# Running a router's gelu, logits, softmax and top-2 picks inside attention, in nine groups of tiles

## The reference

```python
x = layernorm(x + attention(x))       # 4 heads of 64, rotary embedding, causal softmax, output projection
# router, on the tokens xf of the normed x
ri = concat([xf, stats(xf)], -1)      # mean, std, min, max, l2 norm, share of near-zeros: 262 columns
h = gelu(ri @ r1_w.T + r1_b, approximate=False)     # 128 hidden columns
probs = softmax(h @ r2_w.T, -1)                     # 32 experts
topp, topi = top_k(probs, 2)
wnorm = topp / topp.sum(-1)                         # the two gates of a token
score = where(routed, probs, -inf)
idx = argsort(-score, axis=0)[:320].T               # each expert takes its 320 best tokens
out = sum over experts of w * down(silu(gate) * up) of the gathered tokens, plus a grouped adapter
x = layernorm(x + out)
```

## Time and profile before

| what | us |
|---|---|
| three runs, median (lowest to highest) | 2360.45 (2357.5 to 2361.66) |
| the profiled execution, its own time | 2361.54 |
| its span, first to last instruction | 2359.6 |
| PE busy over the span | 1971.2 |
| DVE busy | 1491.6 |
| ACT busy | 1331.8 |
| POOL busy | 823.7 |
| granted PE clock, mean over the span | 0.922 |

### The profile page before, as it was taken

The page is one execution under the profiler, slowest core; times in us unless marked ns, Lnnn a source line. Parts: engine busy times, 40 slices in busy tenths (PEclk is TensorE's granted clock), DMA queues, the critical chain, the costliest instruction groups (busy, mean ns, idle before and its releaser), DMA issues. The chain is left out here.

```text
span 2359.6 us, 43734 instructions
## 1 busy us (share of the span) xinstructions
PE 1971.2 (84%) x14340; PEld 1794.1 (76%) x14340; DVE 1491.6 (63%) x3318; ACT 1331.8 (56%) x3381; POOL 823.7 (35%) x937
## 2 busy tenths in 40 slices
PE   5799999999999999999999987501176999999990
PEld 5699988888988888988888876500155999999990
DVE  6655566656566656666666775288864666666655
ACT  4666665666665666665666653200065666666655
POOL 1122333333333333333111110000095666766652
PEclk9999999999999999999999998555598999999995
DMA  1000011001001001000000110300002444454428
GB/s 60 27 10 21 21 30 32 24 28 33 21 30 32 24 28 32 22 30 28 23 26 24 32 32 21 147 0 0 0 0 83 149 143 134 149 167 150 149 52 285
DMA packets 91405, 135.81 MB, mean 58 GB/s; under 512 B 16932, under 2 KB 79376, under 8 KB 87148
## 3 DMA queue, kind: packets, MB, share of 16 engines
q1 hardware_dynamic: 75372, 123.52, 15.2%
q0 software_dynamic: 15872, 10.24, 2.6%
HBM read 104.62 MB, written 39.85 MB: 61 GB/s over the span
## 5 line engine op out<-in xcount | busy, mean ns | idle before, releaser
L474 PE MATMUL out_ps<-v_sb,probs_t 128*128 128x64 f32 x4352 | 551.0, 271 | 17.6 <-DVE attn L773 15.1
L474 PEld LDWEIGHTS out_ps<-v_sb,probs_t 128*128 128x128 f32 x4352 | 532.4, 194 | 27.4 <-DVE probs_t L750 20.6
L736 DVE TENSOR_REDUCE part_max<-scores_ps 128x1 f32<-128x512 f32 (+3 forms) x576 | 356.9, 621 | 205.0 <-PE scores_ps L439 148.8
L611 ACT ACTIVATE probs<-scores_ps,neg_max 128x512 f32<-128x512 f32 (+3 forms) x640 | 398.1, 627 | 45.0 <-DVE neg_max L740 42.7
L439 PE MATMUL scores_ps<-k_st,q_parts 128*128 128x512 f32 (+3 forms) x1280 | 410.8, 403 | 11.4 <-ACT probs L611 5.0
L456 PE MATMUL probs_t_ps<-ident,probs 128*128 128x128 f32 x2176 | 347.6, 275 | 1.0 <-DVE probs_t L750 1.0
L620 ACT COPY probs_t<-probs_t_ps 128x512 f32<-128x512 f32 (+3 forms) x416 | 208.5, 501 | 244.6 <-PE probs_t_ps L456 243.2
L456 PEld LDWEIGHTS probs_t_ps<-ident,probs 128*128 128x128 f32 x2176 | 261.4, 142 | 51.4 <-issue 2.6
L1463 PE MATMUL up_ps<-xe_t,w 128*128 128x320 f32 x1920 | 288.9, 310 | 2.4 <-DVE xe_t L1570 1.7
L1463 PEld LDWEIGHTS up_ps<-xe_t,w 128*128 128x128 f32 x1920 | 283.6, 189 | 3.0 <-issue 1.9
L439 PEld LDWEIGHTS scores_ps<-k_st,q_parts 128*128 128x128 f32 x1280 | 200.5, 193 | 25.2 <-ACT probs L611 7.2
(11 more groups left out here) (214 smaller groups left out, 3153.8 us busy)
## 6 DMA issues: line engine op xcount, KB each, us to landing
w_raw<-in_w_expert SPq DMA_DIRECT2D x32, 1536.0 KB, 6.4
w_raw<-in_w_adapter SPq DMA_DIRECT2D x32, 384.0 KB, 6.9
x_t<-in_x_t SPq DMA_DIRECT2D x64, 128.0 KB, 2.1
x_row<-in_x SPq DMA_DIRECT2D x64, 128.0 KB, 2.0
x_rows<-x SPq DMA_DIRECT2D x64, 128.0 KB, 1.7
acc_rows<-x SPq DMA_DIRECT2D x64, 128.0 KB, 1.8
ln_x<-acc_rows SPq DMA_DIRECT2D x16, 512.0 KB, 6.2
out_rows_dram<-ln_y SPq DMA_DIRECT2D x16, 512.0 KB, 5.2
```

The costliest lines, as they stand in the source:

```text
L474: mm = pe.matmul(o_ps[:, h, :], probs_t[:, g % PT_RING, a - lo:a - lo + P], v_sb[:, slot(b, a // P), h, :], start=a == 0, stop=a == t * P)
L611: act.activation(probs[:, g % PROBS_RING, 0:hi - lo], s_ps[:, g % AHEAD, 0:hi - lo], ACT.Exp, bias=neg_max[:, u % 8:u % 8 + 1], accum_out= ...
L736: red = dve.tensor_reduce(neg_max[:, ring:ring + 1] if single else part_max[:, ring, c:c + 1], s_ps[:, g % AHEAD, 0:hi - lo], AX.X, ALU.ma ...
```

## The change

The router's part from gelu to the two gates leaves `route` and becomes steps of attention. `token_groups` cuts the order of tiles into nine groups of 8, 4, 8, 8, 8, 8, 8, 8 and 4 tiles. When the last tile of a group has passed `hidden_read`, ACT runs `gelu` on the whole group (in one instruction of up to 128 x 1024), and PE runs `logits` into `misc_ps` (two instructions for each tile). DVE reads them (`logits_read`), ACT takes the exponential (`chances`), and DVE goes through `share`, `first`, `first_hit`, `second`, `second_hit` and `gates`, one step in each of the following slots, on up to 128 x 256 elements each. By the lists of slots the logits of the nine groups come in slots 127, 163, 247, 323, 407, 483, 563, 623 and 641, and the gelu in slots 126, 161, 245, 321, 405, 481, 562, 622 and 641. The last group has no chunks beside it: all its steps stand at the end of the stage.

The hidden columns are no longer stored to DRAM or loaded back. `routed`, `gate` and `best_w` (the rank of each pick) stay on chip between the stages. The masks `hit1` and `hit2` are rebuilt in `route` from the ranks: POOL subtracts, and ACT takes the absolute value and a relu of one minus it. The ring of probabilities has 6 places instead of 8. The scratch tiles `junk` and `squares` go; their writers use `work` and `absolute`, with a drain on ACT between L667 and L668. SP loads the router's two weights at the start of attention.

In `route` the stores and loads of hidden columns, the gelu (L1063), the logits (L1093), the exponential (L1067) and all DVE work from L1151 to L1197 are taken out; `memset unit` goes from DVE to POOL, and DVE waits for `hits_ready` before L1264.

```diff
@@ -51,9 +51,10 @@
 ONE = 1
 
 AHEAD = 4
-PROBS_RING = 8
+PROBS_RING = 6
...
+GROUP = 8
...
@@ -140,18 +143,39 @@
                     continue
                 if k.endswith("_read") and made[k[:-5], of] < at:
                     early[at].append((k, of))
+                    made[k, of] = at
                 else:
                     made[k, of] = at
                     late[at].append((k, of))
+            for j, tiles in enumerate(groups):
+                if tiles[-1] == s - 2 and r == len(ROUNDS) - 2:
+                    late[at].append(("gelu", j))
+                elif tiles[-1] == s - 2 and r == len(ROUNDS) - 1:
+                    late[at].extend((("logits", j), ("logits_read", j)))
+                    picked[j] = at
...
+    for j, at in picked.items():
+        for n, k in enumerate(("chances", "share", "first", "first_hit", "second", "second_hit", "gates")):
+            late[min(at + 1 + n, total + 2)].append((k, j))
...
+def token_groups(order):
+
+    groups = []
+    for m, (b, t) in enumerate(order):
+        if m == 0 or len(groups[-1]) == GROUP or order[m - 1][1] == 4 and t == 3:
+            groups.append([])
+        groups[-1].append(m)
+    return groups
...
-        hidden = sb("hidden", [P, 2, 2, P])
+        hidden = sb("hidden", [P, GROUP, P])
+        w_r2 = sb("w_r2", [P, E])
+        b_r1 = sb("b_r1", [P, 1])
+        rank_e = sb("pick_rank", [P, E])
+        chance, work, hit, left = (sb(f"pick_{n}", [P, GROUP, E]) for n in ("chance", "work", "hit", "left"))
+        top = sb("top", [P, 4, GROUP])
...
             sp.dma_start(w_raw[0:NSTAT, W_R1S:W_END], dram["w_r1s"]).then_inc(weights_loaded, 16)
+            sp.dma_start(w_r2[:], dram["w_r2"]).then_inc(router_loaded, 16)
+            sp.dma_start(b_r1[:], dram["b_r1"]).then_inc(router_loaded, 16)
...
+                elif kind == "logits":
+                    claim("logits", shifted, k + 1)
+                    if k == 0:
+                        pe.wait_ge(router_loaded, 32)
+                    pe.wait_ge(gelu_done, k + 1)
+                    for n, m in enumerate(groups[k]):
+                        mm = pe.matmul(m_ps[:, places[m] * E:(places[m] + 1) * E], hidden[:, n, :], w_r2[:],
+                                       start=True, stop=True)
+                    mm.then_inc(logits_done, 1)
...
                     row = x1[:, k % 2, 0:D]
-                    act.activation(squares[:], row, ACT.Square, accum_out=powers_of[:, 1:2])
+                    act.activation(absolute[:], row, ACT.Square, accum_out=powers_of[:, 1:2])
+                    act.drain()
                     act.activation(absolute[:], row, ACT.Abs).then_inc(abs_ready, 1)
...
-                    act.wait_ge(hid_done, j + 1)
-                    if j >= 2:
-                        act.wait_ge(hid_stored[j % 2], 32 * (j // 2))
-                    act.copy(hidden[:, j % 2].rearrange("p a b -> p (a b)"), m_ps[:, D:2 * D]).then_inc(hid_copied, 1)
+                    act.wait_ge(hid_done, k // 2 + 1)
+                    j = group_of[k]
+                    n = groups[j].index(k - 1)
+                    if n == 0 and j:
+                        act.wait_ge(logits_done, j)
+                    act.copy(hidden[:, n:n + 2].rearrange("p a b -> p (a b)"), m_ps[:, D:2 * D])\
+                       .then_inc(hid_copied, 1)
+                elif kind == "gelu":
+                    if k == 0:
+                        act.wait_ge(router_loaded, 32)
+                    act.drain()
+                    part = hidden[:, 0:len(groups[k])].rearrange("p a b -> p (a b)")
+                    act.activation(part, part, ACT.Gelu, bias=b_r1[:]).then_inc(gelu_done, 1)
+                elif kind == "chances":
+                    act.wait_ge(shifted, k + 1)
+                    part = chance[:, 0:len(groups[k])].rearrange("p a b -> p (a b)")
+                    act.activation(part, part, ACT.Exp).then_inc(chances_ready, 1)
...
-                    dve.scalar_tensor_tensor(junk[:], absolute[:], SPARSE_EPS, part[:].to_broadcast([P, D]),
+                    dve.scalar_tensor_tensor(work[:].rearrange("p a b -> p (a b)"), absolute[:], SPARSE_EPS, part[:].to_broadcast([P, D]),
                                              ALU.is_lt, ALU.mult, accum_out=x1[:, r, D + 5:D + 6])
                     dve.drain()
...
+                chance_, work_, hit_, left_ = (x[:, 0:n] for x in (chance, work, hit, left))
+                m1, best1, best2, total = (top[:, a, 0:n] for a in range(4))
+                ranks = rank_e[:].unsqueeze(1).to_broadcast([P, n, E])
+                if kind == "logits_read":
+                    dve.wait_ge(logits_done, j + 1)
+                    logits = m_ps[:, 0:n * E].rearrange("p (a e) -> p a e", e=E)
+                    dve.tensor_reduce(m1, logits, AX.X, ALU.max)
+                    dve.drain()
+                    dve.tensor_tensor(chance_, logits, wide(m1), ALU.subtract).then_inc(shifted, 1)
+                elif kind == "share":
+                    dve.wait_ge(chances_ready, j + 1)
+                    dve.tensor_reduce(total, chance_, AX.X, ALU.add)
+                    dve.drain()
+                    dve.reciprocal(total, total)
+                    dve.drain()
+                    dve.tensor_tensor(chance_, chance_, wide(total), ALU.mult)
+                    dve.drain()
+                elif kind in ("first", "second"):
+                    best = best1 if kind == "first" else best2
+                    among = chance_ if kind == "first" else left_
+                    dve.tensor_reduce(best, among, AX.X, ALU.max)
+                    dve.drain()
+                    dve.tensor_tensor(work_, among, wide(best), ALU.is_equal)
+                    dve.drain()
+                    dve.tensor_tensor(work_, work_, ranks, ALU.mult)
+                    dve.drain()
+                    dve.tensor_reduce(m1, work_, AX.X, ALU.max)
+                    dve.drain()
+                elif kind == "first_hit":
+                    put(j, best_w, m1, 0)
+                    dve.tensor_tensor(hit_, work_, wide(m1), ALU.is_equal)
+                    dve.drain()
+                    dve.scalar_tensor_tensor(left_, hit_, -2.0, chance_, ALU.mult, ALU.add)
+                    dve.drain()
+                elif kind == "second_hit":
+                    put(j, best_w, m1, 1)
+                    dve.tensor_tensor(work_, work_, wide(m1), ALU.is_equal)
+                    dve.drain()
+                    dve.tensor_tensor(work_, hit_, work_, ALU.add)
+                    dve.drain()
+                    dve.tensor_tensor(chance_, chance_, work_, ALU.mult)
+                    dve.drain()
+                    for b, t0, t1, n0, n1 in runs[j]:
+                        dve.scalar_tensor_tensor(routed[:, t0:t1, b, :], work_[:, n0:n1], 1.0, chance_[:, n0:n1],
+                                                 ALU.subtract, ALU.add)
+                elif kind == "gates":
+                    dve.tensor_tensor(total, best1, best2, ALU.add)
+                    dve.drain()
+                    dve.reciprocal(total, total)
+                    dve.drain()
+                    dve.tensor_tensor(best1, best1, total, ALU.mult)
+                    dve.tensor_tensor(best2, best2, total, ALU.mult)
+                    dve.drain()
+                    put(j, gate, best1, 0)
+                    put(j, gate, best2, 1)
+                    dve.drain()
+
+            def put(j, to, x, a):
+                for b, t0, t1, n0, n1 in runs[j]:
+                    dve.tensor_copy(to[:, t0:t1, b, a], x[:, n0:n1])
 
             for g in range(AHEAD):
...
                     n += 1
             pool.sem_inc(lane_copied, ONE)
+            pool.memset(unit[:], 1.0).then_inc(consts, 1)
+            wait(pool, consts, 7, pool_passed)
+            ranks = rank_e[:].unsqueeze(1).to_broadcast([P, NTT, E])
+            for k, hit in enumerate((hit1, hit2)):
+                own = best_w[:].rearrange("p a b k -> p (a b) k")[:, :, k:k + 1].to_broadcast([P, NTT, E])
+                pool.tensor_tensor(hit[:].rearrange("p a b c -> p (a b) c"), ranks, own, ALU.subtract)\
+                    .then_inc(rank_off, 1)
...
         @block.scalar
         def _(act):
-            act.wait_ge(loaded, 32)
-
-            for b in range(NTT // 16):
-                act.wait_ge(hid_loaded[b], 16 * G)
-                for g in range(G):
-                    part = hpre[:, (g * TG + 4 * b) * P:(g * TG + 4 * b + 4) * P]
-                    act.activation(part, part, ACT.Gelu, bias=b_r1[:]).then_inc(gelu_done, 1)
+            act.wait_ge(consts, 7)
+            for k, hit in enumerate((hit1, hit2)):
+                act.wait_ge(rank_off, k + 1)
+                flat = hit[:].rearrange("p a b c -> p (a b c)")
+                act.activation(flat, flat, ACT.Abs)
+                act.drain()
+                act.activation(flat, flat, ACT.Relu, scale=-1.0, bias=unit[:]).then_inc(hits_ready, 1)
```

(26 more changed lines are left out.)

113 lines of the change are left out of this document (24 added, 89 removed).

## The result

The changed kernel takes 2402.73 us (median, 2395.81 to 2406.58); the kernel before took 2361.05 us in the same rounds. The ratio is 1.0174, with a 95% interval from 1.0143 to 1.0205: 1.7% slower. I had forecast 2353.5 us, faster, and a range that ended at 2385. The sign was wrong and the time lay outside the range.

The account below looks back on a forecast made before the run. Attention was taken as bound by PE, 96% busy, with a serial stretch after it. 69 - (15 + 9 + 33 + 5) = 7 us saved gave 2353.5 us; 8-in-10 range 2320 to 2385.

Parts of the forecast that it names:

- What route saves, 69 us: Between the last hidden copy and the transposes of `routed`: PE's transposes start at 1497.0 instead of 1565.75; bounds 65 and 71.
- The masks rebuilt in the route, nothing: In route, POOL's subtractions and ACT's activations take under 20 us together, needed some 130 us later, so cost nothing.
- PE, 15 us: In attention, 120 logits instructions beside chunks at 0.125 us each cost PE 15 us; ends 13 and 26.
- ACT, 9, and DVE, 33: In attention, ACT's gelu and table loads cost 9 us (0 to 29), DVE's picks 33 us (10 to 73).
- Clock: ... I take 2 in all: In attention, PE is less busy in stretched slots, so the lower clock costs 2 us in all.
- drain 1 us, ring nothing: In attention, the ACT drain in each `stats` costs 1 us; a ring of 6 never fills and costs nothing.
- The clock: Rival: each group's idling lowers attention's clock, PE loses 40 us for eight groups instead of 2; 2391 us; chance 0.10.
- DVE becomes the bound of its slots: Rival in attention: only half of DVE's 38 us takes picks, DVE term 52, net 12 us lost, 2372; chance 0.25.
- nearly all is hidden: Rival: in attention only PE's instructions and some 5 us are paid; 49 us saved, 2311 us; chance 0.18.
- With all upper ones it loses some 75: Whole kernel: with every term at its upper end the change loses some 75 us; these do not come together.
- The second rule, collisions of DVE and POOL: In attention, two-input DVE picks and POOL's SBUF reads exclude each other: 2 us, or 17 if half the steps are struck.
- The first rule, the drain of a table load: On ACT in attention, 1.38 us more per table switch, up to 22 us, perhaps 7 on PE; left out.

Follow-up runs that it names:

- the spread kernel: Changed kernel with the picks cut into seventeen short steps, spread over more slots and mostly kept off those with attention-chain steps; 2374.32 us, ratio 1.0064.
- the one with sixteen tiles and no gelu: Changed kernel with picks made in route, five groups (16, 16, 16, 12, 4 tiles) and Relu in place of Gelu; 2352.69 us, ratio 0.9969.
- the kernel with late picks and no gelu: Changed kernel with both picks of all tiles made in route and Relu in place of Gelu; 2339.94 us, ratio 0.9909.
- late picks and the gelu kept: Changed kernel with both picks of all tiles made at once in route; gelu, logits and exponential stay in attention; 2375.07 us, ratio 1.0064.

## Why the prediction was wrong, step by step

- *What route saves, 69 us.* Right: 69.25. Chain, constants and order as priced.
- *The masks rebuilt in the route, nothing.* Right within 1.3 us. POOL's two subtractions of 2048 columns take 3.7 us each, inside the bound, and lie beside the search.
- *PE, 15 us.* Right for the instructions: with gelu and picks out of the way the logits' rows sum to 16.4 us, some 14.5 of them in attention. In the changed kernel they are 18.7, because part of them runs at the lower clock.
- *ACT, 9, and DVE, 33: 42 us of waits.* PE's idle time grew by 49.4. The kernels split it: gelu 9.8 to 13.8, picks 31 to 35. Both terms were near for what they priced, a wait. In the group that I had walked, ACT's stop was foretold as 1.9 us and came as 2.18. For `second` I had 1.9 and it was 3.08 against 0.90 before, 2.2 more. So the discounts on DVE's free time (38 us usable, 5.6 of lag) were about due in their sum. The places were right only in part, so some of this is luck: of the 35 us of waits that the picks bring without gelu, 5 stand behind the transposed rows and 8 at the scores behind the exponentials, as foretold; 9 each stand behind DVE's copies of probabilities and behind `attn_t`.
- *Small ones: "Clock: ... I take 2 in all".* **This is the step that failed.** It measured 37.5 us on the matmuls that were there before, and 4.2 more on the logits (18.7 - 14.5). From the start to 25 us before the last `hidden` copy, the trace has the granted clock at 1.2 GHz for 124.5 us, where the kernel before has 37.5. Then 2 us become about 42, the waits come out 7 above, and 2353.5 turns into about 2400. The sign that I had named for it fits: the clock of attention is 0.95, under 0.96. The rows behind the 2 us were clocks of the kernel before; none of them said what new waits and new matmuls would do to the clock.
- *Small ones: drain 1 us, ring nothing.* Too low as well: together 7.7 us, with an interval from 3.8 to 10.4, in the run with these two alone.
- *The rivals.* "The clock" had 0.10 and is the one that came. It has PE idle for some 5 us more in each group's slots, measured 49.4 / 8 = 6.2; and 40 us for slow matmuls, from the earlier trace rows, measured 37.5 and 4.2. Its 2391 is 12 us short, mostly by the 7 us of waits and by these 4.2. That its price came so near is partly luck: from kernel to kernel the half rate does not follow the waits, as the spread kernel and the one with sixteen tiles and no gelu show. "DVE becomes the bound of its slots" had a term of 52, and the picks cost 53, but 18 to 22 of these are slower matmuls and not waits, so it has the number without the mechanism. The rival "nearly all is hidden" is out.
- *The ends.* "With all upper ones it loses some 75" does not come out of the terms: 69 - (26 + 29 + 73 + 5) is a loss of 64.
- *The second rule, collisions of DVE and POOL.* I took 2 us, because L813 never went over 427 ns in the earlier trace rows. The picks do. Groups of the changed kernel by line and form:

```profile
L929 DVE TENSOR_TENSOR pick_work<-pick_hit,pick_work 128x256 f32<-128x256 f32 x7 | 3.0, 425 | 0.5
L931 DVE TENSOR_TENSOR pick_chance<-pick_chance,pick_work 128x256 f32<-128x256 f32 x7 | 4.2, 603 | 0.6
L923 DVE SCALAR_TENSOR_TENSOR pick_left<-pick_hit,pick_chance 128x256 f32<-128x256 f32 x7 | 4.1, 590 | 0.5
```

and the longest, from the timeline:

```profile
1407.28 1.35 DVE L931 TENSOR_TENSOR pick_chance<-pick_chance,pick_work 128x256 f32<-128x256 f32 x1
...
1407.09 1.26 POOL L983 TENSOR_TENSOR q_parts<-q_t,q_parts 128x512 fp32r<-128x512 f32 x1
```

  DVE's instruction ends 0.28 us after POOL's, as if it had stood still meanwhile: 1.35 - 0.42 = 0.93 us. This is what the Trainium skill says (SBUF — State Buffer, SBUF: two separate sides): of a DVE instruction with two SBUF inputs and a POOL one that reads SBUF, whichever starts first has the shared ports to its end. Over L913 to L934 the means of the forms lie above 425 ns by 5.3 us in all: more than 2, far from 17. L813 was a poor witness: even in the changed kernel the same line has no instance over 427 ns, while others, in other places, have. L801 of the earlier trace rows, which I passed over for its median, was the better one: in the kernel before, 19 of its 64 instances take over 600 ns, and beside each of them POOL is at work on L849 or L858.
- *The first rule, the drain of a table load.* Rightly left out: in the timeline above each load is 1.28 us and the next activation starts 0.01 us behind it.

What stays open: what brings the clock down in each place; how much of the half rate would stay if the same waits were cut into smaller ones everywhere (the spread kernel has 78.5 us of it, the changed one 124.5); and the 6 to 8 us of the small parts, of which the trace shows 4.

## What to carry to other kernels

In a stretch bound by TensorE, give a side task three prices: its own matmuls, the waits it brings, and what all matmuls lose when the clock falls to its lower level. The last can be as large as the waits (here 41.7 us against 49.4), but it is no fixed share of them: 19.3 us of scattered waits went with 1.6 us of it, and elsewhere 9.6 us came with no wait more. Spread a side task in single short steps, away from those that feed TensorE next, and read the clock of the stretch in every version. Gathering it into fewer and longer blocks made the gelu cheaper and the rest dearer, with nothing gained in all. With two suspects, run all four combinations: when the differences add up, as here, each cost is known.

## What the hardware showed that I had not expected

The clock also fell where PE did not wait. In the kernel with late picks and no gelu, from 814 to 828 us PE has no wait at all, and yet:

```profile
812.00:816.00 4.00, 4.00 (x37) 3.69 (x36) 3.60 (x9) 3.79 (x9) 1.50 (x3) 1.00 0.20 68
816.00:820.00 4.00, 4.00 (x29) 3.71 (x28) 2.13 (x10) 3.04 (x10) 1.72 (x2) 0.78 0.10 31
820.00:824.00 4.00, 4.00 (x20) 3.70 (x19) 1.98 (x4) 1.16 (x4) 0.00 (x0) 0.50 0.00 0
824.00:828.00 4.00, 4.00 (x25) 3.60 (x25) 1.75 (x4) 1.58 (x3) 1.17 (x1) 0.86 0.02 6
```

What lies ahead of the fall is the logits of group 3 (816.45 to 818.37): sixteen matmuls of 32 columns in 1.92 us, behind sixteen of 64 in 1.90. The granted clock is at its lower level, 1.2 GHz, from 818.3 to 825.2 us. In this kernel one group of eight has such a dip near its logits. With late picks and the gelu kept, six of eight have one within 7 us. In three of them it lies already under the logits themselves, which then take 3.57 us in place of 1.92 (twice), or 1.86 in place of 1.03 in the group of four tiles. What in these stretches brings the clock down was not tested alone.
